# Three accumulating scatters moved in between the gathers of the second batch, on the queue of GpSimd

## The reference, cut to what matters

```python
probs = softmax(x @ gate_w)                    # B=2, T=1024, E=8
top_p, top_idx = top_k(probs_et, cap)          # cap = 256 tokens for each expert
xin = take_along_axis(x[:, None], top_idx[..., None], axis=2)
h = gelu(einsum('BElC,ECH->BElH', xin, w1))    # C=128, H=512
y = einsum('BElH,EHC->BElC', h, w2) * top_p[..., None]
out = zeros.at[b_idx, top_idx].add(y)
x = layernorm(x + out)
```

## Time and profile before

| | us |
|---|---|
| median of 3 runs | 915.82 (915.28 to 916.74) |
| the profiled execution | 917.63 |
| its span, first to last instruction | 915.6 |
| TensorE busy | 872.7 (95% of the span) |
| ScalarE busy | 726.6 (79%) |
| VectorE busy | 662.7 (72%) |
| GpSimd busy | 624.3 (68%) |

### The profile page before, as it was taken

How to read it: one execution, slowest core, us unless ns; L and a number is a source line. 1 busy time by engine, 2 the same in 40 slices (tenths; PEclk the granted TensorE clock), 3 DMA queues, 4 the chain that set the end, 5 groups by cost and what they waited for, 6 DMA issues and landing times.

```text
span 915.6 us, 14690 instructions
## 1 busy us (share of the span) xinstructions
PE 872.7 (95%) x4574; PEld 731.3 (80%) x4576; DVE 662.7 (72%) x1105; ACT 726.6 (79%) x1397; POOL 624.3 (68%) x1012
## 2 busy tenths in 40 slices
PE   6889999999999999999999999999999999988695
PEld 5668888888888888888888888888888887777594
DVE  5777777777777777777777767779898886475044
ACT  3888888888888888888888988888888887544234
POOL 1777767767676767677778766767766677757751
PEclk9999999999999999999999999999999999999798
DMA  6011110202020201001010200000000003432251
GB/s 179 13 44 39 38 45 5 77 1 82 1 81 1 70 13 58 12 19 52 1 29 1 68 9 19 14 18 15 19 13 18 1 18 99 120 71 34 45 94 46
DMA packets 44845, 36.16 MB, mean 39 GB/s; under 512 B 6192, under 2 KB 42576, under 8 KB 44512
## 3 DMA queue, kind: packets, MB, share of 16 engines
q1 hardware_dynamic: 40864, 31.69, 11.8%
q0 software_dynamic: 3904, 3.54, 2.7%
HBM read 24.86 MB, written 14.55 MB: 43 GB/s over the span
## 4 chain that ended last, share of the span: by engine, by line
PE 86%; POOL 3%; ACT 3%; DVE 3%; issue 3%; another core or an unknown queue 1%; DMA 0%; SPq 0%; POOLq 0%; DVEq 0%; ACTq 0%
PE t_ps L1536 11%; PE ring_a L1497 6%; PE ring_a L1499 6%; PE ring_a L1498 6%; PE ring_b L1497 6%; PE ring_b L1499 6%; PE u_ps L1497 6%; PE ring_b L1498 6%; PE u_ps L1499 6%; PE u_ps L1498 6%; PE ring_a L1800 3%; PE o_ps L1497 3%; PE o_ps L1498 2%; PE o_ps L1499 2%; PE ring_b L1813 2%
## 5 line engine op out<-in xcount | busy, mean ns | idle before, releaser
L656 POOL TENSOR_TENSOR attn<-prob 128x1024 f32<-128x1024 f32 x128 | 307.6, 2403 | 173.8 <-ACT prob L797 162.1
L1036 DVE TENSOR_TENSOR at_lo<-t_ps,at_hi 128x512 fp32r<-128x512 f32 x253 | 174.0, 688 | 100.7 <-ACT at_hi L780 100.4
L1029 DVE TENSOR_REDUCE negmax<-ring_a 128x1 f32<-128x1024 f32 x128 | 156.7, 1224 | 59.6 <-PE ring_a L1499 56.7
L780 ACT ACTIVATE at_hi<-t_ps 128x512 fp32r<-128x512 f32 x253 | 151.6, 599 | 40.0 <-PE t_ps L1536 39.0
L1029 DVE TENSOR_REDUCE negmax<-ring_b 128x1 f32<-128x1024 f32 x128 | 156.1, 1219 | 2.8 <-PE ring_b L1499 1.2
L1536 PE MATMUL t_ps<-ident,attn 128*128 128x128 f32 x1012 | 152.2, 273 | 4.3 <-DVE at_lo L1036 4.1
L797 ACT ACTIVATE prob<-prob,coef 128x1024 f32<-128x1024 f32 x128 | 147.6, 1153 | 5.7 <-POOL coef L620 5.6
L1536 PEld LDWEIGHTS t_ps<-ident,attn 128*128 128x128 f32 x1012 | 124.8, 140 | 29.9 <-DVE at_lo L1036 9.0
L791 ACT ACTIVATE prob<-ring_a,negmax 128x1024 f32<-128x1024 f32 x128 | 143.1, 1118 | 4.5 <-DVE negmax L1029 4.1
L791 ACT ACTIVATE prob<-ring_b,negmax 128x1024 f32<-128x1024 f32 x128 | 142.4, 1113 | 0.6 <-DVE negmax L1029 0.5
L1497 PE MATMUL ring_b<-xt_hi,q_hi 128*128 128x512 f32 x256 | 112.0, 437 | 0.0
(11 more groups left out here) (431 smaller groups left out, 1634.9 us busy)
## 6 DMA issues: line engine op xcount, KB each, us to landing
w_copy<-in_L_ffn_w SPq DMA_DIRECT2D x16, 256.0 KB, 3.6
q_hi<-w_copy SPq DMA_DIRECT2D x8, 256.0 KB, 3.0
q_lo<-w_copy SPq DMA_DIRECT2D x8, 256.0 KB, 6.4
ww_dram<-ww_hi SPq DMA_DIRECT2D x8, 192.0 KB, 2.5
ww_dram<-ww_lo SPq DMA_DIRECT2D x8, 192.0 KB, 2.8
ww_hi<-ww_dram SPq DMA_DIRECT2D x8, 192.0 KB, 2.4
ww_lo<-ww_dram SPq DMA_DIRECT2D x8, 192.0 KB, 2.5
wq_s<-in_L_attn_Wq SPq DMA_DIRECT2D x8, 128.0 KB, 3.3
```

Source lines behind the costliest of these rows:

```text
L656: pool.tensor_tensor(attn[:, t % AB, :], prob[:, t % 2, 1, :], prob[:, t % 2, 0, :], ALU.add).then_inc(attn_ready, 1)
L780: act.activation(at_hi[:, g % 2, half * GT:(half + 1) * GT, c], t_bank(t, half)[:, :].rearrange("p (k q) -> p k q", q=P), ACT.Copy).then_i ...
L1029: dve.tensor_reduce(negmax[:, par, m:m + 1], ring[m][:, :], axis=AX.X, op=ALU.max, negate=True).then_inc(negmax_ready, 1)
L1036: dve.tensor_tensor(at_lo[:, g % 2, k, c], t_bank(t, half)[:, :].rearrange("p (k q) -> p k q", q=P), at_hi[:, g % 2, k, c].bitcast(F32), A ...
```

## The change

Scatters 4, 5 and 6 of batch 0 move from behind the 16 gathers of batch 1 to places between them. The new order on GpSimd is: gathers of jobs 8 to 11 (eight DMAs), scatter 4, gathers of job 12 (two), scatter 5, gathers of jobs 13 and 14 (four), scatter 6, gathers of job 15 (two), then scatters 8, 7 and 9. Scatter 8 now stands behind scatter 6. Every scatter keeps its own waits. No other line changes.

```diff
@@ -739,7 +739,13 @@
             for q in range(E, JOBS):
                 for k in range(CT):
                     gather_rows(q, k)
-            for q in (4, 5, E, 6, 7, E + 1):
+                if q == E + 3:
+                    scatter(4)
+                if q == E + 4:
+                    scatter(5)
+                if q == E + 6:
+                    scatter(6)
+            for q in (E, 7, E + 1):
                 scatter(q)
             for b in range(B):
                 ln_pows_end(b)
```

## The result

| | kernel before | changed kernel |
|---|---|---|
| median, us | 915.55 (914.83 to 916.74, 4 runs) | 905.27 (903.93 to 907.75, 4 runs) |
| ratio | | 0.989, interval 0.9865 to 0.9914 |
| profiled execution | 917.63, span 915.6 | 905.88, span 904.2 |

The change is 10.3 us faster. The forecast was 918.4 us, so it had the wrong sign. The time lies inside the range of 903 to 921, next to the rival that ends at 903.9. One execution of the kernel before, at 1536 us, fell far out of line with a granted clock of 0.688 and is in no ratio of this document.

What follows compares the result with a forecast made beforehand. Bound by TensorE, with a 22 us stretch where its finished work reaches ScalarE late. Start 0, gathers 0, tail 0, stretch +2.6 us on 915.82 gave 918.4 us; own range 916.5 to 920, wider range 903 to 921.

Steps and rivals of the forecast that it cites:

- the rival that ends at 903.9: Slow stretch in the experts' part breaks at the first moved scatter: 11.9 us faster, 903.9 us, chance 0.20.
- The place and the price of the stretch: From 845.3 to 867.4 us, ScalarE hears late of TensorE's finished work; costs 14.5 us, 0.66 per us.
- A backlog of nine: At the stretch's start, 845.3 us, 15 GpSimd gathers are issued and 5 started, so about 9 wait.
- GpSimd runs dry: Stretch's end at 867.38 us was tied to GpSimd going idle at 867.01; with the change dry at 870.9, 3.9 us later.
- +2.6 us: Cost of a stretch made longer by GpSimd's later idling: 3.9 us at a rate of 0.66.
- The engine's times: GpSimd's new schedule: gathers 1.32 us, scatter DMAs 1.88; scatter 4 at 849.3, scatter 6 at 864.8, free at 870.9.
- The lateness of gathers: Moved gathers of jobs 12 to 15 hidden by 12 us and more behind the stretch, cost 0; uncovered, job 13 late first.
- The tail: Scatters 8, 7, 9 and SyncE's loads at the end: up to 1.8 us sooner, 13 us of slack, gain zero.
- Breaks at the first moved scatter: Rival: TensorE resumes at 846.2 to 849.1, job 13's gather takes 2.7 of 14.5 us back; 903.9 us, chance 0.20.
- The chances: Whole kernel: faster by more than 1.8 us 0.38, slower by more 0.42, the rest 0.20.
- the five cases: Forecast 918.4 us (0.34), same 915.8 (0.20), broken 903.9 (0.20), shortened 909.6 (0.18), longer 925.6 (0.08).

Runs made afterwards that it cites:

- m2_pause: Kernel before, with job 12's gathers waiting for y_scale of job 8's first half so that GpSimd idles; stretch present: 908.07 us, ratio 0.9927.
- j2: Kernel before, with a job's gathers issued only once those of the job two before have landed; stretch present: 911.58 us, ratio 0.9968.
- k2: Kernel before, with scatters 4 and 5 both directly behind the eighth gather; stretch present: 904.23 us, ratio 0.9870.
- k3: The change without scatter 6 among the gathers, against the kernel before; stretch present: 903.03 us, ratio 0.9863.
- k1: Kernel before, with only scatter 4 moved, behind the eighth gather; stretch present: 908.91 us, ratio 0.9925.
- m1: Kernel before, with halves of scatters 4 and 5 behind the gathers of jobs 11, 12, 14 and 15; stretch present: 911.72 us, ratio 0.9963.
- e4_s4_s5: The change without scatter 6 among the gathers, against the kernel before; stretch missing: 903.84 us, ratio 1.0051.
- f1_changed: The changed kernel again, beside the kernel before; stretch missing: 903.82 us beside 900.20, ratio 1.0045.
- j1_changed_third: The changed kernel once more, against the kernel before at 914.29 us; stretch present: 907.14 us, ratio 0.9889.
- f2_before_again: The kernel before, unchanged, measured again for a trace; stretch missing: 901.35 us, ratio 1.0001.

## Why the prediction was wrong, step by step

**The place and the price of the stretch: right.** It was put at 14.5 us from rows of one profile; the kernel before without it is 14.5 us shorter at job 12 and 14.6 over the span. It begins with the same instruction in both kernels, as stated.

**The cause, "GpSimd busy with DMAs issued ahead": half right.** GpSimd's indirect DMAs are needed for it (m2_pause) and not enough: in three measurements the same DMAs ran without it. A backlog of nine isn't needed: with at most four gathers on the way it comes as well (j2). The Trainium skill, page "TensorE: Matmul & The Clock Gate", table of the trn2 specs, gives GpSimd a queue of 8. The first profile has more ahead: at 845.3 us 15 gathers are issued and 5 begun, which leaves ten, not the nine of the prediction; nothing in the sum hangs on it. That a full queue starts the stretch was the prediction's reading of it, and this reading falls: in j2 no more than four gathers wait to land and the late starts are there.

**The end, "GpSimd runs dry": this is the step that failed.** The prediction read one coincidence (867.38 and 867.01) as a rule, and made from it "dry 3.9 us later, so 3.9 x 0.66 = 2.6 us more". In the changed kernel the stretch was over 24 us before GpSimd ran dry, and in j2_rolling_again it ended while the engine went on. In its place the runs show that the order of the same DMAs, on an engine that is just as busy, moves the end and the size of the waits: with scatters 4 and 5 both among the first ten gathers (the change, k2, k3) the late starts are gone by 15.9 to 20.6 us behind the first gather instead of 28.9 (a few come back later in k2), and with one early scatter (k1) or with halves (m1) they aren't. The "+2.6 us" of the sum should have been -10.4 at job 12. Why the order does this is not shown.

It isn't that scatters hold TensorE's word up less than gathers. The longest wait of the first profile, 3.68 us, lies beside the scatters at 859.81 and 861.74:

```profile
858.74 0.60 ACT L866 ACTIVATE attn<-ring_a 128x512 f32<-128x512 f32 x1 [2.51 <-remote]
863.02 0.37 ACT L850 ACTIVATE attn<-ring_b,xg 128x128 f32<-128x128 f32 x1 [3.68 <-remote]
```

`down(15)`, which this `y_scale` needs, is over at 854.51. So the argument that the prediction held against the breaking rival, "in the four scatters it went on", read that trace rightly. What failed was to carry it from scatters behind sixteen gathers to scatters behind eight and ten.

**The engine's times: right up to scatter 6.** With 1.44 us taken off, scatter 4 was due at 847.9, job 12 at 851.7, scatter 5 at 854.3, job 13 at 858.1, scatter 6 at 863.4; they came at 847.84, 851.62, 854.37, 858.17 and 863.55. Behind scatter 6, whose DMAs take 1.92 and 1.72 us, the engine is 0.6 to 1.1 us later than worked out.

**The lateness of gathers: the cover was real, the slack was not 12 us.** Job 13's price of 2.7 us without the cover is what e4_s4_s5 (a wait of 2.67) and f1_changed (2.59) show. With the shortened stretch job 13 was still covered, and job 15 was not quite: 0.20 us here, 1.95 in j1_changed_third, which also waits 0.40 for job 13.

**The tail: right**, nothing in it decides.

**The rivals.** "Breaks at the first moved scatter" gave 903.9 with the right sign and nearly the size. Its mechanism holds in part: TensorE resumed at `up(16)` at 847.67, on the old kernel's clock 849.11, which is where the old kernel resumes too (849.14) and so no sign of a break, and the delay wasn't gone before 850; the last late start is at 857.65, and job 12 came at 859.79, on the old kernel's clock 861.2, past the 857.1 to 860 it gave. The late gather of job 13 took nothing back (863.52 is 3.73 us behind 859.79), because it lay under the rest of the stretch. So the near hit of 903.9 is partly luck: it is 14.5 us off for a stretch gone at once and 2.7 back, where the runs have 10.4 off and nothing back.

**The chances.** 0.38 stood on faster, 0.34 on a forecast that rested on one coincidence of ends. That 905.3 lies within 903 to 921 says little, because this range spans four of the five cases. None of the five cases had that the stretch may be missing altogether; then the change is 3.6 us slower, and for another reason than the forecast gave.

**What stays open.** By which path GpSimd's work holds up TensorE's signals, why it does so in some measurements and not in others (both kinds came up under one and the same chip number), why two early pairs of scatters end it early, while one pair (k1) only makes it milder and single scatter DMAs (m1_halves) change little, and why the scatters alone from 869.26 on in the earlier trace rows have none of it. One piece can be placed: the traces also hold the times of the semaphore updates. In the first profile that of `down(13)`, over at 845.29, stands at 847.25, and that of `down(15)`, over at 854.51, at 862.99, each 0.03 us ahead of ScalarE's start, while ScalarE's own updates stand 0.01 us behind its ends. So the delay lies between TensorE's matmul (whose end is modelled) and its update, and not in ScalarE. GpSimd isn't slower with the stretch: its gathers take 1.01 us in both kinds.

## What to carry to other kernels

Two events that end together once in one trace are a coincidence until a second place in the trace has them too; ask it for the opposite case before a term of the sum rests on it. Where a profile has waits that it can put down to no instruction, measure the unchanged kernel again at another time before tuning around them: here the same edit is 1.1% faster with them and 0.45% slower without. When DMAs of different urgency share one in-order engine, work out for each transfer when it is asked for with no disturbance (31.7 us for job 15, 22.4 for job 13) and place the others in that slack.

## What the hardware showed that was not expected

In four of seven measurements, while GpSimd worked on a series of gathers and scatters, ScalarE waited up to 4.4 us for word of finished TensorE instructions (j2, 859.38), while GpSimd's gathers kept their 1.01 us and ScalarE's instructions their 0.37 and 0.60. In the kernels profiled with it the first late start came 7 to 12 us behind the first gather (in the resumed series of m2_pause after 5 to 7 us), and it was gone about 1 us after GpSimd stopped.

What it leaves of TensorE, by the windows of the kernel before in its first profile (window, its us, busy us and instructions of PE, PEld, DVE, ACT and POOL, granted clock, DMA share, GB/s):

```profile
845.00:870.00 25.00, 15.59 (x72) 12.92 (x71) 0.00 (x0) 6.04 (x15) 18.18 (x17) 0.80 0.27 44
```

and the same window of the same code in f2_before_again:

```profile
845.00:870.00 25.00, 24.75 (x168) 22.88 (x168) 6.24 (x14) 11.87 (x26) 19.86 (x17) 1.00 0.28 45
```

TensorE has 15.6 us of work against 24.75, and a granted clock of 0.80 against 1.00. POOL and the DMA share are nearly the same in both: neither GpSimd's load nor the traffic of the DMAs tells the two apart.
